# Cross attention over the batch: the product row of the last query batch on GpSimd instead of VectorE

## The reference, cut to what matters

```python
ln1 = _layer_norm(hidden_states, ln1_weight, ln1_bias)      # S=8 here, B=512 tokens, H=256
qkv = jnp.einsum('sbh,oh->sbo', ln1, qkv_weight)            # 16 query heads of 16, 4 key/value heads
scores = jnp.einsum('bgqsd,bgtd->bgqst', qb, kb) * scale    # s, t: batches, 8 x 8 for each token
scores = jnp.where(causal, scores, finfo.min)               # query batch s sees key batches t <= s
attn = jax.nn.softmax(scores, axis=-1)
ao = jnp.einsum('bgqst,bgtd->bgqsd', attn, vb)
h1 = hidden_states + ao @ proj_weight.T
```

## Time and profile before

| | us |
|---|---|
| median of 3 runs | 2836.78 (2836.17 to 2840.8) |
| the profiled execution | 2835.08 |
| its span | 2833.1 |
| busy TensorE / VectorE / ScalarE / GpSimd | 2706.5 / 1727.5 / 1378.7 / 820.5 |
| the stage of cross attention | 2194.8 to about 2443 |

### The profile page before, as it was taken

One profiled execution on the slowest core, in us unless ns is written; L12 is line 12 of the kernel. 1 busy time (PEld: TensorE's weight loads), 2 busy tenths in 40 slices (PEclk: granted clock), 3 DMA queues, 4 the chain that ended last, 5 costly groups with the idle time before them and its releaser, 6 DMA issues. The chain is left out here.

```text
span 2833.1 us, 50970 instructions
## 1 busy us (share of the span) xinstructions
PE 2706.5 (96%) x19124; PEld 1808.2 (64%) x19124; DVE 1727.5 (61%) x5112; ACT 1378.7 (49%) x3081; POOL 820.5 (29%) x830
## 2 busy tenths in 40 slices
PE   7999999887999999999999999999999887899998
PEld 4667776654566666666666666666666444578886
DVE  5888887778766555556565656566745788711113
ACT  4777777524554545555555454545541332322224
POOL 1001111124433332323232333333331210045551
PEclk9999999998999999999999999999999988999999
DMA  6544443325545455545455555454540000123325
GB/s 191 134 122 109 120 124 105 100 75 173 162 120 158 134 167 158 159 126 168 139 168 152 149 155 149 145 156 129 145 124 26 12 16 30 60 68 82 74 76 200
DMA packets 241380, 344.48 MB, mean 122 GB/s; under 512 B 25635, under 2 KB 174118, under 8 KB 237024
## 3 DMA queue, kind: packets, MB, share of 16 engines
q1 hardware_dynamic: 232304, 320.71, 39.0%
q0 software_dynamic: 7680, 16.32, 2.3%
q10 hardware_dynamic: 1152, 4.19, 0.4%
HBM read 184.61 MB, written 152.67 MB: 119 GB/s over the span
## 5 line engine op out<-in xcount | busy, mean ns | idle before, releaser
L1664 PE MATMUL bank<-w,gT 128*128 128x256 f32 x2048 | 463.5, 382 | 2.6 <-ACT gT L1582 2.6
L1631 PE MATMUL bank<-h2T,w 128*128 128x512 f32 x1024 | 444.7, 592 | 0.0
L1664 PEld LDWEIGHTS bank<-w,gT 128*128 128x128 f32 x2048 | 383.8, 190 | 75.9 <-issue 24.9
L1582 ACT ACTIVATE gT<-bank,vec 128x512 f32<-128x512 f32 x256 | 175.9, 687 | 389.6 <-PE bank L1631 389.6
L1631 PEld LDWEIGHTS bank<-h2T,w 128*128 128x128 f32 x1024 | 194.6, 190 | 231.3 <-issue 229.6
L1216 POOL TENSOR_TENSOR prob<-prob,rsum 128x512 f32<-128x512 f32 (+1 forms) x256 | 233.2, 933 | 212.7 <-DVE rsum L1428 211.6
L510 DVE CUSTOM_DVE_ANT_0 y<-bank,mask 128x128 f32<-128x128 f32 (+3 forms) x512 | 219.6, 484 | 64.5 <-PE bank L746 64.1
L649 ACT ACTIVATE y<-y,least 128x128 f32<-128x128 f32 (+3 forms) x512 | 248.4, 560 | 10.7 <-DVE least L510 10.6
L1405 DVE CUSTOM_DVE_ANT_0 prob<-bank,mask 128x256 f32<-128x256 f32 (+1 forms) x512 | 164.3, 387 | 124.3 <-PE bank L1619 124.3
L1523 ACT ACTIVATE prob<-prob,least 128x256 f32<-128x256 f32 (+1 forms) x512 | 238.7, 469 | 1.8 <-DVE least L1405 1.8
L1602 PE MATMUL bank<-wtok,hT 128*128 128x512 f32 x512 | 225.3, 592 | 2.1 <-ACT hT L1514 1.3
(11 more groups left out here) (337 smaller groups left out, 4862.9 us busy)
## 6 DMA issues: line engine op xcount, KB each, us to landing
probT<-turned_probs SPq DMA_DIRECT2D x64, 768.0 KB, 5.0
turned_probs<-prob_blocks SPq DMA_DIRECT2D x128, 256.0 KB, 5.5
probT<-turned_probs SPq DMA_DIRECT2D x32, 1024.0 KB, 5.9
turned_rows<-score SPq DMA_DIRECT2D x252, 128.0 KB, 2.9
score<-turned_rows SPq DMA_DIRECT2D x63, 512.0 KB, 3.9
turned_probs<-wide_blocks SPq DMA_DIRECT2D x128, 192.0 KB, 3.1
turned_probs<-prob_blocks SPq DMA_DIRECT2D x128, 192.0 KB, 3.1
w<-in_W SPq DMA_DIRECT2D x8, 1024.0 KB, 8.4
```

Of the source, the lines that this page charges most:

```text
L1582: nc.scalar.activation(gT[:, m, :], M[m % 2][:, :], ACT.Gelu, bias=vec[:, h // B, 4 * KD + m:4 * KD + m + 1])\
L1631: ins = nc.tensor.matmul(M[m % 2][:, :], w1[:, k, m * P:(m + 1) * P], h2T[:, k, :], start=(k == 0), stop=(k == KD - 1))
L1664: ins = nc.tensor.matmul(M[i][:, (t % 2) * D:(t % 2 + 1) * D], gT[:, m, t * P:(t + 1) * P], w2[:, m, :], start=(m == 0), stop=(m == MF - 1))
```

## The change

In tiles 1 to 3, VectorE no longer makes the product row of i = 7. GpSimd makes it, with the same shape and operands, in a new function `last_row(p, ch)`, called for both halves between the two rstd functions. It waits for the queries and keys to be copied to SBUF and for `reduced` of the tile before. TensorE's scores and ScalarE's first copy over the keys wait for GpSimd's row as well as for VectorE's. The semaphore is one of an earlier layer, `gated`, counted on from 7 by `Renewed`. Tile 0 is as before.

```diff
--- before.py
+++ after.py
@@ -1857,6 +1857,7 @@
         kT = c.xn[:, :, :].rearrange("p t n -> p (t n)").rearrange("p (t n) -> p t n", n=P)
         pr = c.hT[:, :, :].rearrange("p k n -> p (k n)")[:, 0:B * P].rearrange("p (t n) -> p t n", n=P)
         S = c.bank[:, 4:6, :].rearrange("p i (t n) -> p (i t) n", n=P)
+        last_products = Renewed(s["gated"], B - 1)
         M = [c.bank[:, 6, :], c.bank[:, 7, :]]
 
         def rows_of(i, ch, t0, n):
@@ -1933,6 +1934,17 @@
                     steps(nc.gpsimd.tensor_tensor(shift2[:, :], mv2[:, :, 0], rstd2[:, :], ALU.mult))
                     nc.gpsimd.tensor_scalar(shift2[:, :], shift2[:, :], -1.0, None, ALU.mult)\
                       .then_inc(s["norm_rstd"], 1)
+
+            def last_row(p, ch):
+                if ch == 0:
+                    drained(pool, ("QKV", (2, 1), p))
+                    drained(pool, ("QKV", (0, 1), p))
+                    pool.wait_ge(s["reduced"], p)
+                else:
+                    drained(pool, ("QKV", (1, 1), p))
+                i = B - 1
+                nc.gpsimd.tensor_tensor(rows_of(i, ch, 0, i + 1), qT[:, ch, i:i + 1, :].to_broadcast([P, i + 1, P]),
+                                        kT[:, 0:i + 1, :], ALU.mult).then_inc(last_products.sem, 1)
 
             nc.gpsimd.memset(ones_of[:, :, :], 1.0)
             nc.gpsimd.memset(spread[:, :, :], 1.0)
@@ -1972,6 +1984,9 @@
             for p in range(NT):
                 if p + 2 < NT:
                     rstd_of(p + 2)
+                if p < LAST_TILE:
+                    for ch in range(2):
+                        last_row(p + 1, ch)
                 rstd2_of(p)
             c.p_steps = steps.done
 
@@ -2003,7 +2018,7 @@
                     drained(dve, ("QKV", (0, 1), p))
                 else:
                     drained(dve, ("QKV", (1, 1), p))
-                for i in (2, 3, 0, 1, 4, 5, 6, 7):
+                for i in (2, 3, 0, 1, 4, 5, 6) if p else (2, 3, 0, 1, 4, 5, 6, 7):
                     if p and ch == 0 and i in (0, 2):
                         full(dve, ("AV", i // 2, p - 1))
                     if p and ch == 0 and i == 4:
@@ -2192,6 +2207,8 @@
                 turns, window, gaps = gaps_of(p)
                 taken(turns)
                 act.wait_ge(s["products_ready"], 2 * p + 2)
+                if p:
+                    last_products.wait(act, 2 * p)
                 taken(window[:2])
                 act.wait_ge(s["cross_shifted"], p + 1)
                 nc.scalar.activation(sm[:, :, :], sm[:, :, :], ACT.Exp, scale=float(HDM) ** -0.5)\
@@ -2277,6 +2294,8 @@
                 else:
                     pe.wait_ge(s["aux"], 5)
                 pe.wait_ge(s["products_ready"], 2 * p + ch + 1)
+                if p:
+                    last_products.wait(pe, 2 * (p - 1) + ch + 1)
                 for par, t0 in ((1, 0), (1, 4), (0, 0)):
                     for j in range(4):
                         i = B // 2 + j if par else B // 2 - 1 - j
```

## The result

| | before | after |
|---|---|---|
| median of 6 runs, us | 2836.48 (2835.5 to 2840.9) | 2854.2 (2848.72 to 2856.15) |
| ratio | | 1.0055, interval 1.0045 to 1.0065 |
| profiled execution, its span | 2835.08, 2833.1 | 2855.24, 2853.5 |

The change makes the kernel slower by 0.55% (the two medians alone differ by 17.7 us, 0.62%). Forecast was 0.37%, 2847.3 us. By the ratio the forecast's 2836.78 us become 2852.4, just inside the range; the median itself, 2854.2, lies 1.2 us over its upper end.

A forecast was written before the change was run, and what follows sets the result against it. A chain from VectorE's half 0 products through TensorE's scores and projections was taken as the bound; +8.5 us in three turns plus 2.0 for TensorE's clock made +10.5, so 2847.3 us, range 2838 to 2853.

The forecast's parts named there:

- Exclusion, one instruction each: Products of half 0: VectorE and GpSimd exclude each other instruction by instruction; each GpSimd row costs VectorE 2.09 us.
- The price of a row: One GpSimd product of 128x1024: 2.38 us taken, ends 1.89 and 2.73; the skill's figure gave an estimated 2.25.
- d = +3.1 us: Delay of the end of half 0's products each turn: VectorE loses 4.2 us and is spared 1.13.
- Turn one: Cross attention, from tile 0 to 1: +3.1 us, on a chain without slack.
- Rival 3: Same mechanism, dearer: GpSimd's blocks over 2.73 us or TensorE longer at the lower clock; +14 to +18 us, chance 0.07.
- Turn two: Cross attention, from tile 1 to 2: +3.1 us, the last addition following the last projection.
- Turn three: Cross attention, from tile 2 to 3: +2.3 us, plus 2.0 for projection and scores at TensorE's lower clock.
- half 1: Second channel half's products: 1.13 us shorter on VectorE, off the chain except in turn three, giving back 0.8 us.
- Rival 1: GpSimd shut out until VectorE's additions from PSUM: turns +1.2, -1.1, -0.8, sum -0.7; 2836.1 us, not slower; chance 0.14.
- it becomes 2845.6: Whole kernel: the profiled execution of 2835.08 us plus 10.5 us from the turns.

The follow-up runs named there:

- experiment 1: Changed kernel, GpSimd writing its rows by memsets instead of multiplying: the three turns together 56.76 us (62.26 before, 72.60 changed), one run 2833.04 us against 2836.14.
- experiment 2: Changed kernel, GpSimd making only the row of half 0, VectorE all eight of half 1: turns together 66.88 us, one run 2841.37 us against 2836.14.
- experiment 3: Kernel before, plus two GpSimd products a turn into an unread scratch tile, no engine waiting: turns together 76.98 us, one run 2853.52 us against 2836.14.
- experiment 7: Changed kernel, GpSimd's rows in turns two and three alone, begun after VectorE's seven of half 0: ratio 0.9985 with idle TensorE products, 0.9990 without.
- experiment 6: Idle TensorE products added: kernel before, turns 59.61 us, ratio 1.0001; changed kernel, turns 66.30 us, one run 2842.38 us against a median of 2838.64.
- experiment 4: Changed kernel, both GpSimd rows begun only after VectorE's seven of half 0: turns together 60.55 us, one run 2834.01 us against 2836.14.

## Why the prediction was right, point by point

- *Exclusion, one instruction each.* Right. The sizes were taken from the earlier trace rows, 2.09 us for one GpSimd row; measured 2.15 (8.60 - 4.30 = 4.30 for two). Experiments 1 to 3 tell it from everything else that the change adds. The prediction put the rule of the Trainium skill, SBUF — State Buffer, "Who interferes with whom", too narrowly: the page counts VectorE's two-port modes among what contends as well, and says that `tensor_tensor` has none, so for these products nothing changes.
- *The price of a row.* 2.38 us taken, 2.35 measured where nothing disturbs it (the first row in experiment 7). The estimate of 2.25 from the Trainium skill, GPSIMD Engine Reference, section 3.1, was 0.1 below; by it the forecast would have been 6 x 0.13 = 0.8 us smaller, not 0.6. The price of the row matters only through what VectorE loses by it.
- *d = +3.1 us.* 3.17 measured in every turn.
- *Turn one.* Forecast +3.1, measured +3.93. The forecast kept the scores and projections behind as they were, but TensorE's granted clock was 0.83 on average over the projections, which took 4.41 us instead of 3.72. Rival 3 named this as a tail and gave the longer idle time as its reason. The length alone doesn't decide it: the projections took 3.73 us after 8.96 us idle (experiment 2) and 3.84 after 12.29 (experiment 3), but 4.33 after 8.00 (experiment 7).
- *Turn two.* Forecast +3.1, measured +2.07. The scores behind projection 1 had run at the lower clock before (3.26 us) and now ran at full (2.15). I hadn't counted that, and it doesn't follow the idle time either: these scores took 2.14 us after 5.53 us idle (experiment 1), 2.88 after 7.68 (experiment 2), 2.15 after 9.83 (the change) and 3.00 after 10.96 (experiment 3).
- *Turn three.* Forecast +4.3, measured +4.34: 3.17, the slow projection 1.8, scores 0.2, less 0.8 of half 1. The chain went over to TensorE as foreseen. That turns of +3.93 and +2.07 add up to nearly the forecast's two times 3.1 is luck: two misses of 0.8 and 1.0 us with opposite signs. With TensorE at full clock in both kernels the turns differ by 6.7 us (experiment 6), so 3.7 of the 10.34 hang on the clock, for which the forecast had 2.0.
- *Rival 1* (GpSimd shut out) is refuted by the rows that stood still. Its arithmetic for late rows came close in experiment 4 in turns one and three (+1.37 and -0.83 against +1.2 and -0.8); the sum, -1.7 against -0.7, differs by turn two's scores at full clock.
- *What was missed.* The sum for the turns was 10.5 and they gave 10.34, but the medians differ by 17.7. The other 7 us lie outside the stage that I looked at. The two profiled executions differ by 10.0 us there: in the table stage (5.5), behind it (1.6) and ahead of the change (3.9), less 1.0 given back. The step that failed is "it becomes 2845.6", which carried everything outside the turns over unchanged. Ahead of the change the instructions are the same, and the start of turn one's last sum lay between 2260.4 and 2268.0 us over all fourteen profiles, 2260.4 to 2267.0 in the four of kernels with all rows on VectorE and 2260.9 to 2268.0 in the ten others, so the 3.9 there can't be put down to the change. Of the table stage I can only say that its clock falls in some executions and not in others. Part of the 7 us may be chance: the kernel before had medians of 2836.48, 2839.04 and 2838.64 us in three sets of runs. Why the rest came with the change stays open.

## What to carry to other kernels

Before work goes from a full VectorE to an idle GpSimd, look for a place in the trace where both run two-input instructions on SBUF and read off how long the VectorE instruction got: here each GpSimd product cost VectorE 2.15 us to spare it 1.13. Work for GpSimd belongs beside VectorE instructions that read PSUM, or it must not read SBUF. And a total can move by more than the stretches that a change touches, here by 7 us on 10, for which no cause was shown: judge the mechanism by those stretches and the time by many runs.

## What the runs showed of the hardware

- GpSimd's memsets of 128x1024 (0.95 us each) beside two-input VectorE products cost these nothing (4.30 us); GpSimd's products cost 2.15 each. The Trainium skill, SBUF — State Buffer, "Who interferes with whom", says that such VectorE instructions contend only with GpSimd instructions that read SBUF; the trace agrees.
- Where both engines have instructions queued they alternate: after one GpSimd product (to 2270.91) exactly one VectorE row ran (to 2271.46), though GpSimd's next had begun at 2270.87 in the profile and then ended at 2273.65. The VectorE row that waits loses the same whatever its size: 2.16 us with 512 elements, 2.14 with 128.
- How long TensorE's granted clock stays at the lower level behind an idle stretch doesn't follow the length of that stretch in these profiles: the same instructions after 8.0 us idle took 3.72 us once and 4.33 us once, and after 12.29 us idle 3.84.
- The granted clock of the same matmuls in the table stage averaged 1.00 in one profile and 0.69 in another, and the stage took 38.39 and 43.92 us. The Trainium skill, TensorE: Matmul & The Clock Gate, part 1, says that the gate's timing runs free of the kernel's start; with that, a shift of what comes before could change where the clock falls. These runs don't contradict it and don't prove it.
